# Attention tables of two heads built in one half: the odd head's and the next even head's

## The chip, the cores and the metric

One core of a Trainium2 chip runs the whole program. The metric is the device time of one execution in microseconds, the median of the runs shown. A step here is one pass of the attention loop, and n counts its (head, sequence) pairs.

## The reference

The input x is 8 sequences of 512 tokens by 128 channels. Three layers follow each other: half a mixture-of-experts layer, attention with 16 heads, and half a mixture-of-experts layer again. The change touches attention alone. For each head h and each sequence:

```python
q, k, v = cproj(Wq), cproj(Wk), cproj(Wv)            # complex, 64 wide
qr, kr = q * phase, k * phase                        # phase: cos and sin of t * omega[h]
E = exp(clip(-mu[h] * |t_i - t_j|, -30, 0))
s = real(qr . conj(kr)); qn = |q|^2; kn = |k|^2
V = sigma_sq/(2 mu) * (1 - E*E) + eta_sq + gamma_sq
maha = max(qn + E*E*kn - 2*E*s, 0) / V
logits = coef[h] * log1p(maha / nu) - 32 * log(V)    # masked to i >= j
out = softmax(logits) @ v                            # then times Wo, added to x
```

E and V depend on the head and on |i - j| alone, so each head has a few tables that serve all 8 sequences: the phases (cos and sin), the decay E, the threshold V (kept as `lam`), and the head's query and key weights split into a high and a low part for the fp32r matmuls.

## The kernel before

Attention is a software pipeline over 16 heads x 8 sequences = 128 pairs, written out in full for every engine. `steps` calls `a_step(i, r)` with n = 16 i + r: i counts pairs of heads, r = 0 to 7 are the steps of the even head 2i (the even half), r = 8 to 15 those of the odd head 2i+1 (the odd half). Scores are lower-triangular: four blocks of 128, 384, 512 and 256 columns lie side by side in 1280 columns (`ORDER`, `OFF`, `SW`).

In step n the engines work on different pairs:

- **TensorE** computes `scores(n)`, the squared norms of pair n+1 (`norms`), the projections of pair n+2 (`project`), turns the probabilities of pair n-1 (`turn`), and multiplies those of pair n-2 with the values (`weigh`). In an even half it also makes the values of both heads of the pair (`values`), 12 more matmuls. An odd half has none of these.
- **VectorE** (in the order of its program): `peaks(n-1)` (L1551, four custom instructions that read `u` and `lam`), half of `accumulate(n-3)` (L1583), `distances(n)` (L1560, which waits for the scores, then L1564), `query_norms(n+1)` (L1570), the other half of `accumulate`, `turn_parts(n+2)` (L1605 and L1607), `inverse(n-1)` (L1575), and last the step's share of the table building.
- **ScalarE**: `soften(n-1)` (L1356), `key_norms(n+1)` (L1364), `clamp(n)` (L1373), `turned_out(n-1)` (L1380), `logs(n)` (L1386), then the table building, `square(n+2)` (L1392) and in even halves `values_out` (L1399).
- **GpSimd**: `rotate(n+1)` (L1482), which waits for the scores of pair n and for the crossing DMA, then `spread(n+1)` (L1491, four pieces in `ORDER`, from `decay` and `knorm` to `ek`).
- **The sync queue** (SP): in every step the two crossing DMAs of pair n+2 (L1146, L1147), issued after L1605; besides these it loads the tables (`load`) and copies the decay (`expand`, L1137).

The table building of head h is placed by the step r mod 8 of the half before it:

```python
        FRONT, EXP, EXPAND, LN, MASK = 1, 2, 3, 4, 6
        def building(part, i, r):
            if r % B != part:
                return None
```

So the tables of an odd head are built in the even half before it, and those of an even head in the odd half before it. FRONT is a copy of the head's parameters (L1509) and dist x (-mu), clipped (L1511). EXP is ScalarE's high part of the weights (L1337) and the exponential (L1340). EXPAND is VectorE's low part of the weights (L1519) and the square of the decay (L1528), and on the sync queue three copies of the widest block of `decay` to the narrower ones. LN is ScalarE's logarithm into `lam` (L1347). MASK is L1535 and L1539 on `lam`. All tables have two buffers, chosen by the parity of the head; those of the even heads lie in the buffer `early`, which the profile prints for several of them.

Of the kernel before, what the change touches and what calls it, by code (L numbers as in the profile page):

```python
# [28 lines left out]
P = 128  # L29
# [1006 lines left out]
def attention_phase(nc, s):  # L1036
# [4 lines left out]
    with ExitStack() as ctx:  # L1041
# [3 lines left out]
        lam = (s.lam0, sb("lam1", [P, N]))  # L1045
        cos = (s.cos0, sb("cos1", [P, N]))
        sin = (s.sin0, sb("sin1", [P, N]))
        hp = (s.hp0, sb("hp1", [P, NPAR]))
# [14 lines left out]
        trig_in = (S["trig_in0"], S["trig_in1"])  # L1063
        block = ctx.enter_context(nc.Block())
# [4 lines left out]
        near = lambda I: slice((TILES - 1 - I) * P, N)  # L1069

# [28 lines left out]
        FRONT, EXP, EXPAND, LN, MASK = 1, 2, 3, 4, 6  # L1099
# [9 lines left out]
        def building(part, i, r):  # L1109

            if r % B != part:
                return None
            if isinstance(i, int) and not 0 < i * 2 + r // B + 1 < H:
                return None
            return r // B + 1

        @block.sync
        def _(sp):
            def load(i, off):
                h, par = i * 2 + off, off % 2  # L1120
                wait(sp, S["w_lo"], h)
                apart(sp, S["sp_passed"])
                wait(sp, S["cos_done"], (h - 1) * B)
                apart(sp, S["sp_passed"])
                sp.dma_start(wqk_raw[:], s.wqk[h]).then_inc(S["w_in"], 16)
# [5 lines left out]
            def expand(i, off):  # L1131

                h, par = i * 2 + off, off % 2
                wait(sp, S["decay_done"], h + 1)
                far = decay[par][:, span(TILES - 1)]
                for I in range(TILES - 1):
                    sp.dma_start(decay[par][:, span(I)], far[:, near(I)]).then_inc(S["expanded"], 16)  # L1137

            def a_step(i, r):
                c = r + 2  # L1140
                if live(i, c):
                    n = i * 16 + c
                    wait(sp, S["rot_done"], n)
                    apart(sp, S["sp_passed"])
                    wait(sp, S["bs_done"], n + 1)
                    sp.dma_start(crossed[0:DH, :], by_sin[DH:P, :]).then_inc(S["crossed_in"], 16)  # L1146
                    sp.dma_start(crossed[DH:P, :], by_sin[0:DH, :]).then_inc(S["crossed_in"], 16)  # L1147
                if building(FRONT, i, r):
                    load(i, building(FRONT, i, r))
                if building(EXPAND, i, r):  # L1150
                    expand(i, building(EXPAND, i, r))

            steps(nc.sync, a_step)
# [176 lines left out]
        def _(a):  # L1330
            def build(part, i, off):

                h, par = i * 2 + off, off % 2
                if part == EXP:
                    a.wait_ge(S["w_in"], h * 16 + 16)
                    wait(a, S["qk_done"], (h - 1) * B)
                    a.activation(wqk[par][0][:], wqk_raw[:], ACT.Copy).then_inc(S["w_hi"], 1)  # L1337
                    a.wait_ge(S["arg_done"], h + 1)
                    far = decay[par][:, span(TILES - 1)]
                    a.activation(far, far, ACT.Exp).then_inc(S["decay_done"], 1)  # L1340
                elif part == LN:
                    if h == 0:
                        a.wait_ge(S["decay_done"], 1)
                        a.activation(decay2[:], decay[0][:, span(TILES - 1)], ACT.Square).then_inc(S["decay2_done"], 1)
                    a.wait_ge(S["decay2_done"], h + 1)
                    wait(a, S["zred_done"], 2 * (h - 1) * B)
                    a.activation(lam[par][:], decay2[:], ACT.Ln, bias=hp[par][:, A_PLUS_B:A_PLUS_B + 1],  # L1347
                                 scale=hp[par][:, NEG_A:NEG_A + 1]).then_inc(S["lnv_done"], 1)
# [11 lines left out]
            def key_norms(i, r):  # L1360
                n, par = i * 16 + r, parity(r)
                wait(a, S["kn_done"], n + 1)
                wait(a, S["ek_done"], n)
                a.activation(knorm[:], s.p6[:], ACT.Identity,  # L1364
                             bias=hp[par][:, NEG_NU_A:NEG_NU_A + 1]).then_inc(S["norm_done"], 1)
# [16 lines left out]
            def logs(i, r):  # L1382
                n, par = i * 16 + r, parity(r)
                for k, (half, _) in enumerate(HALVES):
                    a.wait_ge(S["relu_done"], 2 * n + k + 1)
                    a.activation(u[:, half], u[:, half], ACT.Ln, bias=hp[par][:, U_MIN:U_MIN + 1]).then_inc(S["ln_done"], 1)  # L1386
# [39 lines left out]
            def a_step(i, r):  # L1426
# [14 lines left out]
                if i == 0 and r == -1:  # L1441
                    build(LN, 0, 0)
# [12 lines left out]
                for part in (EXP, LN):  # L1455
                    if building(part, i, r):
                        build(part, i, building(part, i, r))
# [12 lines left out]
        def _(g):  # L1470
            def build_first():
                g.wait_ge(S["lnv_done"], 1)
                apart(g, S["pool_passed"])
                g.tensor_scalar(lam[0][:], lam[0][:], hp[0][:, LAM_SCALE:LAM_SCALE + 1],
                                hp[0][:, NEG_LN_NU:NEG_LN_NU + 1], ALU.mult, ALU.add).then_inc(S["lam0_done"], 1)
# [29 lines left out]
        def _(v):  # L1505
            def build_front(i, off):
                h, par = i * 2 + off, off % 2
                wait(v, S["norm_done"], (h - 1) * B)
                v.tensor_copy(hp[par][:], s.params[:, bass.ds(h, 1), :].rearrange("p a c -> p (a c)")).then_inc(S["hp_done"], 1)  # L1509
                v.wait_ge(S["hp_done"], h + 1)  # L1510
                v.tensor_scalar(decay[par][:, span(TILES - 1)], s.dist[:, span(TILES - 1)], hp[par][:, NEG_MU:NEG_MU + 1],  # L1511
                                MIN_EXP, ALU.mult, ALU.max).then_inc(S["arg_done"], 1)

            def build_weights(i, off):

                h, par = i * 2 + off, off % 2
                v.wait_ge(S["w_hi"], h + 1)
                wait(v, S["qk_done"], (h - 1) * B)
                v.tensor_tensor(wqk[par][1][:], wqk_raw[:], wqk[par][0][:].bitcast(F32),  # L1519
                                ALU.subtract).then_inc(S["w_lo"], 1)  # L1520

            def build_square(i, off):

                h, par = i * 2 + off, off % 2
                far = decay[par][:, span(TILES - 1)]
                v.wait_ge(S["decay_done"], h + 1)
                v.wait_ge(S["lnv_done"], h)
                v.tensor_tensor(decay2[:], far, far, ALU.mult).then_inc(S["decay2_done"], 1)  # L1528

            def build_back(i, off):  # L1530

                h, par = i * 2 + off, off % 2
                if h > 0:
                    v.wait_ge(S["lnv_done"], h + 1)
                    v.tensor_scalar(lam[par][:], lam[par][:], hp[par][:, LAM_SCALE:LAM_SCALE + 1],  # L1535
                                    hp[par][:, NEG_LN_NU:NEG_LN_NU + 1], ALU.mult, ALU.add).then_inc(S["lam0_done"], 1)
                v.wait_ge(S["lam0_done"], h + 1)
                diag = lam[par][:, near(0)]
                v.scalar_tensor_tensor(diag, s.upper[:], hp[par][:, INV_COEF:INV_COEF + 1], diag,  # L1539
                                       ALU.mult, ALU.add).then_inc(S["lam_done"], 1)  # L1540

            def peaks(i, r):
                n, par = i * 16 + r, parity(r)
                v.wait_ge(S["lam_done"], i * 2 + r // B + 1)
                wait(v, S["exp_done"], n)
                wait(v, S["tr_done"], n)
                for k, (_, pieces) in enumerate(HALVES):
                    v.wait_ge(S["ln_done"], 2 * n + k + 1)
                    apart(v, S["dve_passed"])
                    for I in pieces:  # L1550
                        last = v.tensor_tensor_reduce(z[:, span(I)], u[:, span(I)], lam[par][:, near(I)],  # L1551
                                                      hp[par][:, NEG_COEF:NEG_COEF + 1], HIGHEST, ALU.add, ALU.min,
# [13 lines left out]
            def query_norms(i, r):  # L1566
                n, par = i * 16 + r, parity(r)
                wait(v, S["q2_done"], n + 1)
                wait(v, S["relu_done"], 2 * (n - 1))
                v.tensor_scalar(qnorm[:, r % 2, :], s.p5[:, 0:TILES], hp[par][:, NEG_NU_A:NEG_NU_A + 1], None,  # L1570
                                ALU.subtract).then_inc(S["qn_done"], 1)
# [135 lines left out]
            def a_step(i, r):  # L1707
# [27 lines left out]
                if building(FRONT, i, r):  # L1735
                    build_front(i, building(FRONT, i, r))
                if building(EXPAND, i, r):
                    build_weights(i, building(EXPAND, i, r))
                    build_square(i, building(EXPAND, i, r))
                if building(MASK, i, r):  # L1740
                    build_back(i, building(MASK, i, r))
                if i == 0 and r == -1:
                    late_refine()
                if i == 0 and r == 0:
                    build_back(0, 0)
# [15 lines left out]
def program(nc, args, out):  # L1761
    with ExitStack() as ctx:
# [24 lines left out]
        def part(n):  # L1787
# [6 lines left out]
        s.hp0 = part(NPAR)  # L1794
        s.late_var, s.late_root, s.late_rstd, s.late_shift = (part(2 * TILES) for _ in range(4))
# [7 lines left out]
                 "late_stat late_mv late_var late_ln late_root late_rstd late_step late_xn late_xt late_hi late_lo mv_done expanded")  # L1803
# [65 lines left out]
```

## Time and profile before

| | |
|---|---|
| median of 3 runs | 1714.13 us (1711.09 to 1719.28) |
| profiled execution, own time | 1711.93 us |
| its span | 1710.1 us |
| TensorE, share of the span busy | 97% |
| VectorE | 87% |
| ScalarE | 85% |
| GpSimd | 57% |
| mean granted TensorE clock | 0.998 |

The attention loop runs from about 261 to 1494 us of the span. A half is the eight intervals from one L1560 to the next, beginning with the L1560 of its first pair.

### The profile page before, as it was taken

To read this page: it belongs to the slowest core of one execution; us is meant where nothing else is said; L and a number is where in the kernel's file an instruction comes from. 1 tells how busy PE (TensorE), PEld (TensorE's weight loads), DVE (VectorE), ACT (ScalarE), POOL (GpSimd) and SP (SyncE) were. 2 spreads that over 40 slices of the span, in tenths; PEclk is the share of its full clock that TensorE was granted. 3 is DMA by queue.
4 is the path that set the end of the run, shared out by engine and by line. 5 is a ranking of instruction groups with operands and counts; after the bars stand their busy time and mean duration, and the time that the engine had idled before them with its cause. 6 is when DMAs were issued, how large, how long until landed. Compare 5 with 4: busy or idle time off the path is not lost. (4 is left out here: it accounts for less than half of the span.)

```text
span 1710.1 us, 30987 instructions
## 1 busy us (share of the span) xinstructions
PE 1650.9 (97%) x9690; PEld 1334.7 (78%) x9690; DVE 1488.8 (87%) x3380; ACT 1457.8 (85%) x2924; POOL 974.7 (57%) x826
## 2 busy tenths in 40 slices
PE   5999988999999999999999999999999999999998
PEld 4787866877887888788788778878887887777876
DVE  6878887899899989988998998899899989977675
ACT  6677678999999999999999999999998998766765
POOL 3554556565556556655665566556565655345565
PEclk9999999999999999999999999999999999999999
DMA  6000032232222323232322223232222222100000
GB/s 175 1 1 1 1 102 66 67 80 62 75 60 78 78 59 81 57 87 50 87 66 65 72 72 75 51 87 62 75 66 72 66 63 60 25 1 13 13 8 18
DMA packets 49475, 98.21 MB, mean 57 GB/s; under 512 B 8096, under 2 KB 25760, under 8 KB 49312
## 3 DMA queue, kind: packets, MB, share of 16 engines
q1 hardware_dynamic: 49312, 96.23, 22.0%
q8 instruction: 78, 1.28, 0.3%
q14 instruction: 85, 0.70, 0.1%
HBM read 17.95 MB, written 5.24 MB: 14 GB/s over the span
## 5 line engine op out<-in xcount | busy, mean ns | idle before, releaser
L1482 POOL TENSOR_TENSOR early<-early 128x1024 f32<-128x1024 f32 x127 | 303.4, 2389 | 483.3 <-PE pS L1162 258.2
L654 POOL TENSOR_TENSOR hid_lo_d<-hid_d,hid_hi_d 128x512 fp32r<-128x512 f32 x176 | 231.4, 1315 | 218.7 <-ACT hid_hi_d L559 212.1
L1373 ACT ACTIVATE early<-early,qnorm 128x128 f32<-128x128 f32 (+3 forms) x512 | 246.5, 553 | 71.8 <-DVE early L1564 70.6
L1162 PE MATMUL pS<-early 128*128 128x128 f32 (+3 forms) x1024 | 297.6, 433 | 0.3 <-PEq L105 0.3
L1356 ACT ACTIVATE early<-early,nmax 128x128 f32<-128x128 f32 (+3 forms) x512 | 281.2, 560 | 13.4 <-DVE nmax L1551 12.5
L1560 DVE SCALAR_TENSOR_TENSOR pS<-pS,ek 128x1280 f32<-128x1280 f32 x128 | 191.0, 1492 | 60.7 <-PE pS L1162 59.8
L1162 PEld LDWEIGHTS pS<-early 128*128 128x128 f32 x1024 | 164.7, 191 | 96.0 <-issue 61.4
L1491 POOL TENSOR_TENSOR ek<-early 128x128 f32<-128x128 f32 (+3 forms) x256 | 216.3, 878 | 3.8 <-ACT early L1364 2.9
L1491 POOL TENSOR_TENSOR ek<-decay,early 128x128 f32<-128x128 f32 (+3 forms) x256 | 215.5, 876 | 2.4 <-DVE pS L1560 2.4
L1177 PEld LDWEIGHTS pV<-ones,early 128*128 128x128 f32 x1016 | 134.2, 193 | 60.8 <-issue 60.8
L1207 PE MATMUL pS<-ident,early 128*128 128x128 f32 x1280 | 169.0, 275 | 12.4 <-DVE early L1564 8.3
L1207 PEld LDWEIGHTS pS<-ident,early 128*128 128x128 f32 x1280 | 146.0, 142 | 43.3 <-issue 17.7
L559 ACT ACTIVATE hid_hi_d<-hid_d 128x512 fp32r<-128x512 f32 x176 | 111.1, 631 | 60.8 <-DVE hid_d L787 42.8
L1380 ACT ACTIVATE probT<-pS 128x1280 f32<-128x1280 f32 x128 | 157.5, 1231 | 5.8 <-PE pS L1207 5.4
L1285 PE MATMUL p<-val_odd,probT 128*128 128x128 f32 x1280 | 155.3, 277 | 1.3 <-ACT probT L1380 1.3
L1583 DVE SCALAR_TENSOR_TENSOR x_sb<-p,rinv,x_sb 128x128 f32<-128x128 f32 x512 | 153.5, 341 | 1.4 <-PE p L1285 1.4
L1285 PE MATMUL p<-val_even,probT 128*128 128x128 f32 x1280 | 153.5, 275 | 0.0
L1285 PEld LDWEIGHTS p<-val_odd,probT 128*128 128x128 f32 x1280 | 147.9, 192 | 2.4 <-ACT probT L1380 1.6
L1285 PEld LDWEIGHTS p<-val_even,probT 128*128 128x128 f32 x1280 | 148.0, 192 | 0.1
L1551 DVE CUSTOM_DVE_ANT_0 early<-early,lam,hp 128x128 f32<-128x128 f32 (+3 forms) x256 | 131.6, 568 | 10.4 <-ACT early L1386 5.4
L1551 DVE CUSTOM_DVE_ANT_0 early<-early 128x128 f32<-128x128 f32 (+3 forms) x256 | 127.7, 554 | 14.4 <-ACT early L1386 12.7
L1175 PE MATMUL pV<-early,ones 128*128 128x512 f32 x254 | 131.9, 601 | 5.7 <-ACT val_odd L1399 4.0
(395 smaller groups left out, 3953.3 us busy)
## 6 DMA issues: line engine op xcount, KB each, us to landing
early<-early SPq DMA_DIRECT2D x256, 256.0 KB, 3.6
early<-trig_d SPq DMA_DIRECT2D x64, 64.0 KB, 2.0
trig_d<-early SPq DMA_DIRECT2D x3, 1024.0 KB, 6.9
early<-in_w SPq DMA_DIRECT2D x3, 704.0 KB, 8.8
x_sb<-in_x SPq DMA_DIRECT2D x4, 512.0 KB, 8.4
early<-in_wqk SPq DMA_DIRECT2D x16, 128.0 KB, 3.5
cos<-trig_d SPq DMA_DIRECT2D x32, 64.0 KB, 2.2
sin<-trig_d SPq DMA_DIRECT2D x32, 64.0 KB, 2.0
```

The source lines that it names most:

```text
L654: g.tensor_tensor(hid_lo[:, par], hid[:, par], hid_hi[:, par].bitcast(F32), ALU.subtract).then_inc(lo_done, 1)
L1162: last = pe.matmul(s.pS[:, span(I)], rot[:, I * P:(I + 1) * P], rot[:, N:N + (I + 1) * P], start=True, stop=True)
L1207: last = pe.transpose(s.pS[:, col:col + P], z[:, col:col + P], s.ident[:])
L1285: last = pe.matmul(s.p7[:, I * P:(I + 1) * P], turned[:, OFF[I] + J * P:OFF[I] + (J + 1) * P], val[:, J * P:(J + 1) * P], start=(J == 0), ...
L1356: last = a.activation(z[:, span(I)], z[:, span(I)], ACT.Exp, bias=nmax[:, I:I + 1], scale=-1.0, accum_out=rsum[:, r % 4, I:I + 1])
L1373: last = a.activation(u[:, span(I)], u[:, span(I)], ACT.Relu, bias=qnorm[:, r % 2, I:I + 1])
L1380: a.activation(probT[r % 2][:], s.pS[:, 0:SW], ACT.Copy).then_inc(S["trc_done"], 1)
L1482: g.tensor_tensor(rot[:], by_cos[:], crossed[:], ALU.add).then_inc(S["rot_done"], 1)
L1491: last = g.tensor_tensor(ek[:, span(I)], decay[par][:, span(I)], knorm[:, 0:(I + 1) * P], ALU.mult)
L1551: last = v.tensor_tensor_reduce(z[:, span(I)], u[:, span(I)], lam[par][:, near(I)], hp[par][:, NEG_COEF:NEG_COEF + 1], HIGHEST, ALU.add, A ...
L1560: v.scalar_tensor_tensor(s.pS[:, 0:SW], s.pS[:, 0:SW], -2.0, ek[:], ALU.mult, ALU.add).then_inc(S["w_done"], 1)
L1583: last = v.scalar_tensor_tensor(xt, s.p7[:, I * P:(I + 1) * P], rinv[:, r % 4, I:I + 1], xt, ALU.mult, ALU.add)
```

## The change

The tables of both the odd head 2i+1 and the next even head 2i+2 are now built in the steps of the even half (r = 1 to 8, and the load of the phases of the even head at r = 9). Each part has two places, the first for the odd head (`off` 1) and the second for the even head (`off` 2). While the even half runs, its own decay and threshold tables are in use, so the next even head gets `far_even` (512 columns) for the decay and a second `lam` buffer in the first 512 columns of `dist`; the decay is then copied to all four blocks of `decay[0]` at r = 8. The high part of the weights goes from ScalarE to VectorE (a `tensor_copy`, HALF), and the copy of the head's parameters goes: all read `s.params` in place. `peaks`, `key_norms`, `logs` and `query_norms` only change their operands so.

```diff
+        expanded = (S["expanded0"], S["expanded1"])
+        def lam(h):
+            return lam1[:] if h % 2 else lam_even[h // 2 % 2]
+        def far(h):
+            return decay[h % 2][:, span(TILES - 1)] if h % 2 or h == 0 else s.far_even
-        FRONT, EXP, EXPAND, LN, MASK = 1, 2, 3, 4, 6
+        FRONT, EXP, HALF, LOW, SQUARE, LN, MASK = (1, 2), (2, 3), (3, 6), (4, 7), (3, 5), (4, 6), (6, 7)
+        WEIGHTS, TRIG, EXPAND = (1, 5), (1, 9), (3, 8)
         def building(part, i, r):
-            if r % B != part:
-                return None
-            if isinstance(i, int) and not 0 < i * 2 + r // B + 1 < H:
-                return None
-            return r // B + 1
+            for off in (1, 2):
+                if r == part[off - 1] and i * 2 + off < H:
+                    return i * 2 + off
+            return None
...
+            def expand(h):
+                par = h % 2
                 wait(sp, S["decay_done"], h + 1)
+                apart(sp, S["sp_passed"])
+                wait(sp, S["t_done"], 2 * (h - 1) * B)
+                for I in range(TILES - par):
+                    sp.dma_start(decay[par][:, span(I)], far(h)[:, near(I)]).then_inc(expanded[par], 16)
...
-                    a.wait_ge(S["w_in"], h * 16 + 16)
-                    wait(a, S["qk_done"], (h - 1) * B)
-                    a.activation(wqk[par][0][:], wqk_raw[:], ACT.Copy).then_inc(S["w_hi"], 1)
...
-                    wait(a, S["zred_done"], 2 * (h - 1) * B)
+                    wait(a, S["zred_done"], 2 * (h - (1 if h % 2 else 3)) * B)
...
-                wait(g, S["expanded"], 48 * (i * 2 + r // B))
+                wait(g, expanded[par], 48 * (i + r // 16 + 1) if par else 64 * (i + r // 16))
...
-                v.tensor_copy(hp[par][:], s.params[:, bass.ds(h, 1), :].rearrange("p a c -> p (a c)")).then_inc(S["hp_done"], 1)
+                    wait(v, expanded[0], 64 * (h // 2 - 1))
...
+            def build_half(h):
+                v.wait_ge(S["w_in"], h * 16 + 16)
+                wait(v, S["qk_done"], (h - 1) * B)
+                v.tensor_copy(wqk[h % 2][0][:], wqk_raw[:]).then_inc(S["w_hi"], 1)
```

## Rows read from the trace of the kernel before

**Rows 1.** Windows, an odd half and the sum of seven: us, then busy (instructions) by engine, clock, DMA.
```profile
core 0: us, PE busy (x) PEld busy (x) DVE busy (x) ACT busy (x) POOL busy (x), PEclk, DMA share, GB/s
496.40:568.60 72.20, 71.18 (x433) 56.05 (x433) 70.49 (x158) 67.07 (x140) 45.60 (x40) 1.00 0.29 74
...
sum 508.90, PE 499.04 PEld 393.07 DVE 496.92 ACT 469.68 POOL 320.23; mean PE 71.29 PEld 56.15 DVE 70.99 ACT 67.10 POOL 45.75
```

**Rows 2.** Windows of the seven even halves between and behind them: the sum.
```profile
sum 560.90, PE 560.75 PEld 472.37 DVE 494.10 ACT 528.50 POOL 320.74; mean PE 80.11 PEld 67.48 DVE 70.59 ACT 75.50 POOL 45.82
```

**Rows 3.** Timeline of VectorE, odd half 496.4 to 568.6: L1560, once a step.
```profile
505.23 1.49 DVE L1560 SCALAR_TENSOR_TENSOR pS<-pS,ek 128x1280 f32<-128x1280 f32 x1
...
514.94 1.48 DVE L1560 SCALAR_TENSOR_TENSOR pS<-pS,ek 128x1280 f32<-128x1280 f32 x1
...
523.63 1.49 DVE L1560 SCALAR_TENSOR_TENSOR pS<-pS,ek 128x1280 f32<-128x1280 f32 x1
...
533.10 1.48 DVE L1560 SCALAR_TENSOR_TENSOR pS<-pS,ek 128x1280 f32<-128x1280 f32 x1
...
541.79 1.49 DVE L1560 SCALAR_TENSOR_TENSOR pS<-pS,ek 128x1280 f32<-128x1280 f32 x1
...
550.67 1.49 DVE L1560 SCALAR_TENSOR_TENSOR pS<-pS,ek 128x1280 f32<-128x1280 f32 x1
...
559.91 1.49 DVE L1560 SCALAR_TENSOR_TENSOR pS<-pS,ek 128x1280 f32<-128x1280 f32 x1
```

**Rows 4.** The same timeline, the first L1551 of the step that begins at 514.94.
```profile
521.22 0.35 DVE L1551 CUSTOM_DVE_ANT_0 early<-early,lam,hp 128x128 f32<-128x128 f32 x1 [0.21 <-issue]
```

**Rows 5.** Single lines of the building: ns minimum/median/maximum of one.
```profile
L1511 DVE TENSOR_SCALAR early<-dist,early x7: 485/487/905, 359.5 to 1274.0; 128x512 f32<-128x512 f32 x7
...
L1519 DVE TENSOR_TENSOR wqk_lo<-early,wqk_hi x15: 389/392/708, 300.4 to 1370.2; 128x256 fp32r<-128x256 f32 x15
...
L1528 DVE TENSOR_TENSOR early<-early x7: 677/679/1219, 377.5 to 1292.2; 128x512 f32<-128x512 f32 x7
...
L1535 DVE TENSOR_SCALAR early<-early x7: 514/517/1014, 404.3 to 1321.5; 128x512 f32<-128x512 f32 x7
...
L1539 DVE SCALAR_TENSOR_TENSOR early<-upper,early x8: 350/352/721, 266.4 to 1322.5; 128x128 f32<-128x128 f32 x8
...
L1347 ACT ACTIVATE early<-early x8: 799/802/813, 258.1 to 1304.6; 128x512 f32<-128x512 f32 x8
```

**Rows 6.** Timelines by engine in an even half, steps from 476.34 and 486.38.
```profile
476.34 1.50 DVE L1560 SCALAR_TENSOR_TENSOR pS<-pS,ek 128x1280 f32<-128x1280 f32 x1 [1.15 <-PE pS L1162]
...
486.38 1.50 DVE L1560 SCALAR_TENSOR_TENSOR pS<-pS,ek 128x1280 f32<-128x1280 f32 x1 [0.71 <-PE pS L1162]
...
478.66 1.93 ACT L1373 ACTIVATE early<-early,qnorm 128x128 f32<-128x128 f32 x4 [0.77 <-DVE early L1564]
...
476.48 2.38 POOL L1482 TENSOR_TENSOR early<-early 128x1024 f32<-128x1024 f32 x1 [4.33 <-PE pS L1162]
```

**Rows 7.** GpSimd and VectorE, odd halves: L1551 beside L1491, and beside L1482.
```profile
838.73 2.38 POOL L1482 TENSOR_TENSOR early<-early 128x1024 f32<-128x1024 f32 x1 [4.76 <-DMA early<-early]
841.07 3.34 POOL L1491 TENSOR_TENSOR ek<-decay,early 128x128 f32<-128x128 f32 x4
...
843.66 0.90 DVE L1551 CUSTOM_DVE_ANT_0 early<-early,lam,hp 128x128 f32<-128x128 f32 x1 [0.21 <-issue]
...
1294.81 2.38 POOL L1482 TENSOR_TENSOR early<-early 128x1024 f32<-128x1024 f32 x1 [1.99 <-DMA early<-early]
...
1294.78 2.69 DVE L1551 CUSTOM_DVE_ANT_0 early<-early,lam,hp 128x256 f32<-128x256 f32 x1
```

**Rows 8.** L1147, issue to landing: all 127, the one at 501.8, the one at 1312.0.
```profile
DMA to landing us min/median/max: 3.6/3.7/5.1
...
DMA to landing us min/median/max: 4.7/4.7/4.7
...
DMA to landing us min/median/max: 5.1/5.1/5.1
```

**Rows 9.** Timeline of the sync queue, the three decay copies of an odd half.
```profile
529.66 2.47 SPq L1137 DMA_DIRECT2D early<-early  x3
```

More of the change, by code:

```diff
@@ L1147, in a_step @@
                     sp.dma_start(crossed[DH:P, :], by_sin[0:DH, :]).then_inc(S["crossed_in"], 16)
-                if building(FRONT, i, r):
-                    load(i, building(FRONT, i, r))
+                if building(WEIGHTS, i, r):
+                    load_weights(building(WEIGHTS, i, r))
+                if building(TRIG, i, r):
+                    load_trig(building(TRIG, i, r))
                 if building(EXPAND, i, r):
-                    expand(i, building(EXPAND, i, r))
+                    expand(building(EXPAND, i, r))
             steps(nc.sync, a_step)
@@ L1330, in _, with build @@
         def _(a):
-            def build(part, i, off):
-                h, par = i * 2 + off, off % 2
+            def build(part, h):
                 if part == EXP:
-                    a.wait_ge(S["w_in"], h * 16 + 16)
-                    wait(a, S["qk_done"], (h - 1) * B)
-                    a.activation(wqk[par][0][:], wqk_raw[:], ACT.Copy).then_inc(S["w_hi"], 1)
                     a.wait_ge(S["arg_done"], h + 1)
-                    far = decay[par][:, span(TILES - 1)]
-                    a.activation(far, far, ACT.Exp).then_inc(S["decay_done"], 1)
+                    a.activation(far(h), far(h), ACT.Exp).then_inc(S["decay_done"], 1)
                 elif part == LN:
@@ L1441, in a_step @@
                 if i == 0 and r == -1:
-                    build(LN, 0, 0)
+                    build(LN, 0)
                 if i == 0 and r == 0:
@@ L1456, in a_step @@
                     if building(part, i, r):
-                        build(part, i, building(part, i, r))
+                        build(part, building(part, i, r))
                 if live(i, r + 2):
@@ L1537, in build_back @@
                 v.wait_ge(S["lam0_done"], h + 1)
[L1538 to L1540 removed]
+                diag = lam(h)[:, near(0)]
+                v.scalar_tensor_tensor(diag, s.upper[:], hp(h, INV_COEF), diag, ALU.mult, ALU.add).then_inc(S["lam_done"], 1)
             def peaks(i, r):
[L1543 removed]
@@ L1550, in peaks @@
                     for I in pieces:
-                        last = v.tensor_tensor_reduce(z[:, span(I)], u[:, span(I)], lam[par][:, near(I)],
-                                                      hp[par][:, NEG_COEF:NEG_COEF + 1], HIGHEST, ALU.add, ALU.min,
+                        last = v.tensor_tensor_reduce(z[:, span(I)], u[:, span(I)], lam(h)[:, near(I)],
+                                                      hp(h, NEG_COEF), HIGHEST, ALU.add, ALU.min,
                                                       nmax[:, I:I + 1])
@@ L1735, in a_step @@
                 if building(FRONT, i, r):
[L1736 to L1739, printed above, removed]
+                    build_front(building(FRONT, i, r))
+                if building(HALF, i, r):
+                    build_half(building(HALF, i, r))
+                if building(LOW, i, r):
+                    build_low(building(LOW, i, r))
+                if building(SQUARE, i, r):
+                    build_square(building(SQUARE, i, r))
                 if building(MASK, i, r):
-                    build_back(i, building(MASK, i, r))
+                    build_back(building(MASK, i, r))
                 if i == 0 and r == -1:
@@ L1794, in program @@
         s.hp0 = part(NPAR)
+        s.far_even = part(N)
         s.late_var, s.late_root, s.late_rstd, s.late_shift = (part(2 * TILES) for _ in range(4))
```

77 lines of the change are left out of this document (34 added, 43 removed).

## The prediction

> **What bounds the kernel now.** I read the windows first, one per half, because the change moves work from one kind of half to the other. The reader is to see that the two kinds have different limits. Seven even halves last 560.9 us, and TensorE is busy for 560.75 of them, 80.1 us a half [rows 2]. VectorE is busy for only 494.1, ScalarE for 528.5. Seven odd halves (those of heads 1 to 13, in which an even head's tables are built) last 508.9 us, 72.7 each, and there VectorE has 496.9, more than in the even halves, though the time is shorter [rows 1]. The last odd half, head 15's, builds nothing and is left out.
>
> The timeline then shows what an odd step costs. In the half from 496.4 to 568.6 the distances between one L1560 and the next are 8.83, 9.71, 8.69, 9.47, 8.69, 8.88, 9.24 and 8.69 us (the outer ends are those of the window) [rows 1, 3]. The three steps of 8.69 build nothing. In them VectorE idles 0.21 us before its first L1551, put down to issue, and nowhere else [rows 4]: this is VectorE's own work, the floor of an odd step. The other steps are longer by what is built in them. In an even step, VectorE instead stands still before L1560 until TensorE's scores are done, 1.15 us where nothing was built in the step before and 0.71 where MASK was [rows 6].
>
> **What the change takes out of the odd halves.** Against 8.69, the steps of that half are longer by 1.02 (FRONT), 0.78 (the low part and the square), 0.19 (ScalarE's logarithm, which delays L1386 and so L1551) and 0.55 (MASK) [rows 3]. The 1.02 is not typical: L1511 takes 905 ns there against its median of 487 [rows 5], 0.42 more, and the parameter copy before it was stretched likewise, so FRONT without such a stretch costs 0.3. That makes 0.3 + 0.78 + 0.19 + 0.55 = 1.8 us a half, 12.7 over seven.
>
> A half at its floor would be 8.83 + 7 x 8.69 = 69.7 us, seven of them 487.6. The trace has 508.9, so the excess is 21.3, of which building explains 12.7. The other 8.6 I read as follows. The crossing DMA L1147 lands after 3.7 us as a rule and after up to 5.1 [rows 8]. Asked one by one, 12 of the 49 that are issued in the first seven steps of these odd halves needed 4.6 or more, the first at 501.8, the last at 1312.0. A late landing makes GpSimd's L1482 and L1491 late. In the step that starts at 837.40, L1491 is at work until 844.41, and the first L1551, due at 843.66, takes 0.90 instead of 0.35; at 1294.8, L1482 is waiting or running when the fourth L1551 should, and that takes 2.69 [rows 4, 7]. So L1551 stands still until GpSimd's instruction ends. The Trainium skill's page "GPSIMD Engine Reference" (Key points) says the same: GpSimd shares its SBUF interfaces with VectorE, and contends with instructions that have two SBUF inputs or run in a 2-port mode. By that rule every building instruction is exposed too, and the trace agrees with 905 ns for L1511, 1219 for L1528 and 1014 for L1535.
>
> Does that 8.6 go as well? Only in part. The large stall of 2.2 us needs L1551 to be late enough to meet the next L1482: it stood in a step that builds. A step without building ends its L1551 before the next landing. But the small stall does not need building; it gets likelier, since GpSimd's start hangs on the landing, and a shorter step leaves less of it over. I keep 12 late landings and give each 0.6 us (0.90 - 0.35 = 0.55 from the row, a bit more for a landing of 5.1): 7.2 us. Seven odd halves then take 487.6 + 7.2 = 494.8, which is 14.1 less than 508.9.
>
> **What it adds to the even halves.** The VectorE shares by step are: r = 1 and 2 FRONT (0.49 each), r = 3 HALF and the square, r = 4 the low part, r = 5 the square, r = 6 HALF and the odd head's MASK, r = 7 the low part and the even head's MASK [rows 5]. The trace has no HALF. It lies between nothing (a step's idle time of 0.31 to 0.4 before L1551 can hide it) and 0.39, the row of the low part with the same 256 columns and two inputs; I take 0.3. The heaviest steps are then MASK plus 0.3 to 0.39. MASK alone brought the idle time before L1560 from 1.15 to 0.71 [rows 6], so 0.3 to 0.4 us is left even at r = 6 and 7, and TensorE does not notice. If this cover were gone, each us would cost 7 us over the halves.
>
> ScalarE loses the copy of the weights and gets a second exponential and a second logarithm, at r = 2, 3, 4 and 6. It waits 0.77 us for L1564 in each even step [rows 6]. The dearest of the four is the logarithm, 0.80 [rows 5], about 0.7 of it additional behind the instruction before it, one per step: hidden. I add nothing for the even halves.
>
> **Queues and waits.** On the sync queue the even head's copies are four instead of three and move from r = 11 to r = 8, where they stand behind that step's crossing DMAs. At 2.47 us for three [rows 9], four take 3.3, and the next crossing is issued 8.7 us after the last: no delay. The copies are first read at r = 15, by L1491. The new waits there (`t_done` of the even head's pairs, `decay_done`) were satisfied before the crossing DMA in front of them was. The weights go to r = 5, behind the low part of r = 4. FRONT's `expanded0` is from the half before. LN at r = 6 waits for the square of r = 5, MASK at r = 7 for that LN, each one step old. TensorE's `project` of the odd head's first pair (r = 6) needs the low part of r = 4, formerly r = 3: still before. All of this costs nothing, and nothing is queued behind a wait that lasts.
>
> **The sum** against the profiled execution's own 1711.9 us: 1711.9 - 14.1 = 1697.8. The median of the runs is 2.2 above it, so 1714.1 - 14.1 = 1700.0 us, 0.8% faster.
>
> **Rivals.**
> *A, GpSimd takes the place (no real change).* At 8.69 us a step, L1482 starts about 0.5 us after L1560 (landing 3.7 after an issue at about 5.5) and L1491 is done 5.7 later, at 6.3, which is just when L1551 starts (521.22 - 514.94 = 6.28 [rows 3, 4]). If landings in a run of short steps are later by 0.2 to 0.3, each step of the odd half would be that much longer: 49 x 0.2 = 10 us given back, 1710. For it speaks that the margin is nil; against it that steps of 8.69 stand right behind others of 8.69 to 8.97, and that a stalled step gives the next one the time back.
> *B, even halves slower (slower than before).* L1482 in an even half starts with the end of the scores (476.48, released by TensorE [rows 6]). If the added work at r = 6 and 7 pushes the last L1551 behind the end of the scores, L1551 is caught by L1482 and stands 2.2 us, as at 1294.8 [rows 7]. Twice in each of seven halves is 31 us: 1700 + 31 = 1731. It decides once the two steps lose more than the 1.1 to 1.3 us between the end of L1551 and L1560; the sum above uses 0.8.
> *C, the excess goes completely.* If late landings no longer meet L1551, 21.3 us are gained: 1693.
> *D, it doesn't do what it says:* the odd step has another floor near by, TensorE, with 71.2 busy of 72.2 [rows 1]. But that busy share stretches with the step; in the 8.69 steps L1560 is not released by TensorE [rows 3].
>
> **Chances.** Forecast 0.62, C 0.14, A 0.14, B 0.07, D 0.03. The forecast's own range is 1696 to 1704. The range for 8 in 10 reaches toward C and into A: 1693 to 1708. What a measurement of this kernel tells from no change is 0.5%, 8.6 us, so under 1705.5 is faster: forecast, C and a tenth of A and D, 0.78; same is most of A and D, 0.14; slower is B and a rest, 0.08.
>
> **What the profile after would show.** Odd halves of 69.7 to 71.5 us in the windows, with VectorE busy near 68.5 and no building line in them; even halves still 80.1 with TensorE busy throughout and VectorE at about 73; the idle time before L1560 at the steps after r = 6 and 7 down to 0.3 to 0.4, but there. The copy HALF near 0.3 us. L1551 durations over 0.35 only in steps behind a late landing. Wrong would be: even steps over 10.05, an L1551 of over 2 us in an even half, L1560 of an odd half released by TensorE or by GpSimd, or landings of L1147 above 4 us at r = 8 and 9, behind the copies.

## The result and the profile after

The changed kernel runs in 1696.9 us (median of 5 runs, 1695.6 to 1700.6), the kernel before in 1715.9 (5 runs, 1711.1 to 1719.6). The ratio is 0.9892, with a 95% interval of 0.9868 to 0.9916: 1.1% faster. The profiled execution took 1695.6 us, 16.3 less than the profiled one of before; 1697.8 was forecast against its own time, 1700.0 for the median.

The page of the kernel after, its first part (engine, busy time, share of the span, instructions):

```profile
span 1693.8 us, 30993 instructions
PE 1642.7 (97%) x9690; PEld 1337.0 (79%) x9690; DVE 1483.9 (88%) x3380; ACT 1452.4 (86%) x2909; POOL 974.3 (58%) x826
```

VectorE has as many instructions as before and 5 us less busy time; ScalarE has 15 fewer, the casts, and also 5 us less. So little work went away; the question is where it lies. The windows of the seven odd halves of the kernel after, with their sum (columns as in [rows 1]):

```profile
495.70:565.40 69.70, 69.70 (x433) 56.45 (x432) 67.62 (x152) 65.11 (x137) 45.59 (x40) 1.00 0.31 79
...
796.00:867.20 71.20, 70.51 (x433) 56.29 (x432) 69.11 (x153) 65.41 (x137) 45.65 (x40) 1.00 0.30 77
...
sum 493.10, PE 491.33 PEld 394.92 DVE 478.15 ACT 457.43 POOL 319.72; mean PE 70.19 PEld 56.42 DVE 68.31 ACT 65.35 POOL 45.67
```

and the sum of the seven even halves between and behind them:

```profile
sum 561.20, PE 561.06 PEld 473.31 DVE 506.20 ACT 533.91 POOL 320.73; mean PE 80.15 PEld 67.62 DVE 72.31 ACT 76.27 POOL 45.82
```

Against [rows 1] the odd halves are 15.8 us shorter and have 18.8 us less of VectorE. Against [rows 2] the even halves have taken on 12.1 us of VectorE and 5.4 of ScalarE, and last as long as before, 561.2 to 560.9. The odd halves are 15.8 of the 16.3 us.

The steps show it best. VectorE's timeline of the half that begins at 495.7, L1574 (L1560 before), where [rows 3] had 9.47, 8.69, 8.88 and 9.24 us between such rows:

```profile
521.92 1.50 DVE L1574 SCALAR_TENSOR_TENSOR pS<-pS,ek 128x1280 f32<-128x1280 f32 x1
530.63 1.49 DVE L1574 SCALAR_TENSOR_TENSOR pS<-pS,ek 128x1280 f32<-128x1280 f32 x1
539.33 1.49 DVE L1574 SCALAR_TENSOR_TENSOR pS<-pS,ek 128x1280 f32<-128x1280 f32 x1
548.03 1.49 DVE L1574 SCALAR_TENSOR_TENSOR pS<-pS,ek 128x1280 f32<-128x1280 f32 x1
```

Now 8.70 follows on 8.70. In the even half, the two fullest steps (r = 6 from 475.63, r = 7 from 485.67), with what VectorE builds in them:

```profile
481.62 0.27 DVE L1531 CAST wqk_hi<-early 128x256 fp32r<-128x256 f32 x1
481.80 0.54 DVE L1550 TENSOR_SCALAR lam<-lam,params 128x512 f32<-128x512 f32 x1
485.67 1.50 DVE L1574 SCALAR_TENSOR_TENSOR pS<-pS,ek 128x1280 f32<-128x1280 f32 x1 [0.49 <-PE pS L1183]
491.66 0.40 DVE L1537 TENSOR_TENSOR wqk_lo<-early,wqk_hi 128x256 fp32r<-128x256 f32 x1
491.97 0.54 DVE L1550 TENSOR_SCALAR early<-early,params 128x512 f32<-128x512 f32 x1
495.70 1.50 DVE L1574 SCALAR_TENSOR_TENSOR pS<-pS,ek 128x1280 f32<-128x1280 f32 x1 [0.36 <-PE pS L1183]
```

The idle time in front of the scores was 1.15 and 0.71 us in [rows 6]; it is down to 0.49 and 0.36, but there: TensorE still releases VectorE, not the other way about.

What is left above 8.70 in the odd halves is the stall that [rows 7] showed, L1565 (L1551 before) behind GpSimd. The longest of the kernel after, GpSimd first, then VectorE:

```profile
833.39 2.41 POOL L1495 TENSOR_TENSOR early<-early 128x1024 f32<-128x1024 f32 x1 [4.96 <-DMA early<-early]
835.73 3.41 POOL L1504 TENSOR_TENSOR ek<-decay,early 128x128 f32<-128x128 f32 x4
...
837.77 0.78 DVE L1565 CUSTOM_DVE_ANT_0 early<-early,lam,params 128x128 f32<-128x128 f32 x1 [0.21 <-issue]
...
838.49 1.07 DVE L1565 CUSTOM_DVE_ANT_0 early<-early,lam,params 128x384 f32<-128x384 f32 x1
```

L1495 waited for a landing that took 5.1 us, L1504 runs to 839.14, and two pieces of L1565 take 0.78 and 1.07 instead of 0.35 and 0.61. Twelve instructions of L1565 in these seven halves are stretched so, by 4.6 us together; none takes more than 1.08, and the 2.69 of [rows 7] has no successor.

### The profile page after: what moved, and what is told of

It reads as the page before. It is cut to its first block and busy times, and to the rows that moved or that the text cites. A ratio compares the mean times of both kernels' runs of the same rounds, so it can differ in the third digit from the quotient of the medians.

```text
span 1693.8 us, 30993 instructions
## 1 busy us (share of the span) xinstructions
PE 1642.7 (97%) x9690; PEld 1337.0 (79%) x9690; DVE 1483.9 (88%) x3380; ACT 1452.4 (86%) x2909; POOL 974.3 (58%) x826
## 3 DMA queue, kind: packets, MB, share of 16 engines
q1 hardware_dynamic: 50320, 98.07, 22.5%
## 5 line engine op out<-in xcount | busy, mean ns | idle before, releaser
L1495 POOL TENSOR_TENSOR early<-early 128x1024 f32<-128x1024 f32 x127 | 303.2, 2387 | 470.0 <-PE pS L1183 258.6
L1574 DVE SCALAR_TENSOR_TENSOR pS<-pS,ek 128x1280 f32<-128x1280 f32 x128 | 191.4, 1495 | 55.3 <-PE pS L1183 54.4
L1504 POOL TENSOR_TENSOR ek<-early 128x128 f32<-128x128 f32 (+3 forms) x256 | 216.7, 881 | 3.6 <-ACT early L1379 3.0
L1504 POOL TENSOR_TENSOR ek<-decay,early 128x128 f32<-128x128 f32 (+3 forms) x256 | 215.3, 876 | 0.0
L1400 ACT ACTIVATE early<-early,params 128x512 f32<-128x512 f32 (+1 forms) x256 | 196.9, 819 | 0.0
L1228 PE MATMUL pS<-ident,early 128*128 128x128 f32 x1280 | 164.5, 274 | 5.1 <-DVE early L1578 3.1
L1565 DVE CUSTOM_DVE_ANT_0 early<-early,lam,params 128x128 f32<-128x128 f32 (+3 forms) x256 | 130.8, 567 | 13.8 <-issue 11.2
```

Of the source, the lines that this page charges most:

```text
L1228: last = pe.transpose(s.pS[:, col:col + P], z[:, col:col + P], s.ident[:])
L1400: a.activation(u[:, half], u[:, half], ACT.Ln, bias=hp(h, U_MIN)).then_inc(S["ln_done"], 1)
L1495: g.tensor_tensor(rot[:], by_cos[:], crossed[:], ALU.add).then_inc(S["rot_done"], 1)
L1504: last = g.tensor_tensor(ek[:, span(I)], decay[par][:, span(I)], knorm[:, 0:(I + 1) * P], ALU.mult)
L1574: v.scalar_tensor_tensor(s.pS[:, 0:SW], s.pS[:, 0:SW], -2.0, ek[:], ALU.mult, ALU.add).then_inc(S["w_done"], 1)
```

## The experiments

All start from the changed kernel. Ratios are to the kernel before, run beside each; the changed kernel itself has 0.9892 (0.9868 to 0.9916). "Odd halves" is the sum over heads 1 to 13, 508.9 us before and 493.1 after; "even halves" the sum over heads 2 to 14, 560.9 and 561.2. The runs were taken in three groups. The median of the kernel before was 1713.7, 1713.8 and 1716.9 us in them, against 1715.9 above, and the changed kernel was not run again in them, so a difference of its 1696.9 from a run of another group is uncertain by some 2 us.

### The placement alone, and a part of it

```diff
-        FRONT, EXP, HALF, LOW, SQUARE, LN, MASK = (1, 2), (2, 3), (3, 6), (4, 7), (3, 5), (4, 6), (6, 7)
-        WEIGHTS, TRIG, EXPAND = (1, 5), (1, 9), (3, 8)
+        FRONT, EXP, HALF, LOW, SQUARE, LN, MASK = (1, 9), (2, 10), (2, 10), (3, 11), (3, 11), (4, 12), (6, 14)
+        WEIGHTS, TRIG, EXPAND = (1, 9), (1, 9), (3, 11)
```

> The changed kernel with the even head's parts put back into the odd half (r = 9 to 14, the decay copies at r = 11); the new buffers, the cast on VectorE and the parameters read in place stay. Theory (the gain is the placement): each odd half gets its building back, about 0.25 + 0.07 + 0.78 + 0.19 + 0.55 = 1.85 us, 13 over seven, and with it some long stalls of L1565: 1710 to 1714, odd halves of 72 to 73 us, even halves 80.1. Rival (one of the other edits made the gain): within 3 us of the changed kernel's 1697, odd halves of 70 to 71.

Measured: 1711.7 us, ratio 0.9983 (0.9966 to 1.0). The windows of the odd halves:

```profile
sum 510.60, PE 500.36 PEld 394.50 DVE 499.04 ACT 467.44 POOL 321.52; mean PE 71.48 PEld 56.36 DVE 71.29 ACT 66.78 POOL 45.93
```

They are back where [rows 1] had them, 510.6 for 508.9, and the even halves still have 561.1. The new buffers, the cast on VectorE and the parameters read in place are all in this kernel and are worth 0.2% together, by the interval at most 0.34%. The placement is the gain.

With only the logarithm and MASK of the even head put back:

```diff
-        FRONT, EXP, HALF, LOW, SQUARE, LN, MASK = (1, 2), (2, 3), (3, 6), (4, 7), (3, 5), (4, 6), (6, 7)
+        FRONT, EXP, HALF, LOW, SQUARE, LN, MASK = (1, 2), (2, 3), (3, 6), (4, 7), (3, 5), (4, 12), (6, 14)
```

> The changed kernel with only the even head's logarithm and MASK back in the odd half (r = 12 and 14). Theory: these steps grow by 0.19 and 0.55 us as before the change, 0.74 x 7 = 5.2: 1701 to 1703. Rival (the gain came from the whole being away, for instance from stalls that any building causes): more than 10 us back, or none.

Measured: 1702.9 us, ratio 0.9941 (0.9921 to 0.9962), odd halves 499.2, which is 6.1 more, for 5.2 expected. The median steps of r = 13 and 14 are 8.88 and 9.25, as before the change, the others 8.70 and the first, r = 8, 8.81, as in the changed kernel. A part put back costs its part.

### The same work added on either side

Four multiplications of 512 columns (0.66 us each) per half, into a spare buffer; in the even halves the condition is `r in (1, 2, 4, 5) and i > 0`:

```diff
+                if r in (10, 11, 12, 13) and i < 7:
+                    wait(v, spare_done, spares[0])
+                    v.tensor_tensor(spare[:], s.dist[:, span(TILES - 1)], s.dist[:, span(TILES - 1)],
+                                    ALU.mult).then_inc(spare_done, 1)
+                    spares[0] += 1
```

> The changed kernel with one more VectorE multiplication of 512 columns, of the kind of the decay's square (0.67 us), into a spare buffer at each of r = 10, 11, 12 and 13 of the seven odd halves of heads 1 to 13. Theory (an odd step is as long as VectorE's own work): each adds 0.6 less the 0.21 of idle time before L1565, so 0.4, 1.6 a half, 11 in all, less up to 3 for late landings that then meet a longer step: 1705 to 1709. Rival (TensorE or GpSimd sets the odd step): 1697 to 1700.

> The same multiplication, as often, at r = 1, 2, 4 and 5 of the even halves of heads 2 to 14. Theory (even halves are TensorE's, VectorE has 0.77 to 1.15 us idle before L1574 in these steps): 1697, no change within 0.2%, even halves still 80.1, that idle time smaller by 0.2 to 0.6. Rival (VectorE's total or its meetings with GpSimd count wherever they are): 1705 to 1709.

In the odd halves: 1707.9 us, ratio 0.9970 (0.9952 to 0.9988), 11.0 above the changed kernel's median; odd halves 505.9 in the profile, with one half of 76.4 to which I come back below. Its median steps are 9.26 at r = 10 and 8.98 at r = 11 to 13, against 8.70 to 8.71: that is 1.4 us a half and 9.7 of the 11. In the even halves: 1699.7, ratio 0.9915 (0.9892 to 0.9937), even halves 561.2. The 2.8 us in the second number are not in the even halves, but that kernel also had three of the multiplications in the steps behind the last pair, which I had not meant. So once more without those:

> The run with extra multiplications at r = 1, 2, 4 and 5 once more, now without the three that also fell into the steps behind the last pair. Theory: the even halves cost nothing, 1697 within 0.2%; what the first run had above 1697 came from those three or from the spread of the runs. Rival (VectorE's work in even halves costs a little, 0.1 us each): 1700.

Measured: 1697.7 us, ratio 0.9885 (0.986 to 0.991), even halves 561.0. The same 28 instructions cost some 10 us in the odd halves and nothing in the even ones. The profiles also show what the three at the end cost. From the last L1577 to the end of the span it is 230.6 us with them and 228.5 without, and 228.6 in the changed kernel (L1574).

### How near the edge r = 7 is

The same multiplication at r = 7, three times and once (`for k in range(3)` or `range(1)` around the lines above, with `r in (7,) and i < 7`).

> The same multiplication three times at r = 7, the fullest step of the even half, in each of the seven even halves before heads 1 to 13. That is 1.8 to 1.9 us more, where 0.36 is left before L1574 and some 0.25 before TensorE's transposes wait. Theory with the stall of rival B (a late L1565 meets L1495, which starts with the end of the scores, and stands until it ends): 1.2 us plus about 2.2 a half, 20 to 25 in all, 1717 to 1722, one L1565 a half of over 2 us. Without such a stall: 1.2 us a half, 1705 to 1706.

> The changed kernel with the 512-column multiplication once, not three times, at r = 7 of the seven even halves before heads 1 to 13: 0.6 us, where 0.36 is left before L1574 and about 0.25 behind it. Theory (rival B decides only where the last L1565 starts behind the end of the scores): nothing to 0.3 us a half, 1697 to 1699, no L1565 over 1.1 us in an even half. Rival (the even half is already at the edge, any more at r = 7 is caught by L1495): 2 us and more a half, 1711 and above.

Three times: 1733.1 us, ratio 1.0109 (1.0082 to 1.0136), slower than before the change. Once: 1697.9, ratio 0.9885 (0.9855 to 0.9914), none of its L1568 over 1.1 us, six of the even halves 0.1 to 0.2 longer each (the step r = 7 takes 10.19 us for 10.04). The step r = 7 from 487.98 of the kernel with three lasts 14.0 us. GpSimd and VectorE in it (L1498 is its L1495, L1507 its L1504, L1568 its L1565, L1577 its L1574):

```profile
498.16 2.41 POOL L1498 TENSOR_TENSOR early<-early 128x1024 f32<-128x1024 f32 x1 [3.83 <-PE pS L1186]
503.67 1.42 POOL L1507 TENSOR_TENSOR ek<-decay,early 128x128 f32<-128x128 f32 x2 [3.10 <-DVE pS L1577]
...
498.26 2.86 DVE L1568 CUSTOM_DVE_ANT_0 early<-early,dist,params 128x512 f32<-128x512 f32 x1
...
501.98 1.48 DVE L1577 SCALAR_TENSOR_TENSOR pS<-pS,ek 128x1280 f32<-128x1280 f32 x1
```

The scores end, GpSimd starts at 498.16 and works until 500.57, and the third L1568, which comes 0.1 us later, ends at 501.12, after 2.86 us where 0.75 is usual. That is rival B, made to happen: it begins between one and three such multiplications, 0.6 and 1.9 us of VectorE's work, away from the changed kernel.

What it costs has two parts. The step r = 7 takes 13.76 us in the median instead of 10.04, 3.7 more for 3.4 expected, or some 26 over seven. The rest is TensorE's clock. In two of the seven halves it stays at 1.00 and the next step is 8.69 us, no longer than in the changed kernel (8.81), although GpSimd waits there too for the late L1577:

```profile
347.22 1.48 DVE L1577 SCALAR_TENSOR_TENSOR pS<-pS,ek 128x1280 f32<-128x1280 f32 x1
355.91 1.49 DVE L1577 SCALAR_TENSOR_TENSOR pS<-pS,ek 128x1280 f32<-128x1280 f32 x1
```

In the other five the granted clock falls and the next step takes 9.70 to 10.90 us, 7 us more in all. Windows in the first of these halves to keep it and in the first to lose it (columns as in [rows 1]):

```profile
348.00:352.00 4.00, 2.28 (x18) 2.06 (x19) 3.96 (x8) 3.17 (x8) 3.09 (x4) 1.00 0.01 4
504.00:508.00 4.00, 3.52 (x18) 3.31 (x19) 4.00 (x8) 3.24 (x6) 3.00 (x4) 0.63 0.02 5
```

26 and 7 make the 33 us by which this profiled execution is longer than that of the changed kernel; the medians differ by 36. The 20 to 25 that were expected had the stall nearly right and the clock not at all.

### Moving a landing, and moving L1565 against it

Two small DMAs ahead of the crossing in the odd steps:

```diff
                     wait(sp, S["bs_done"], n + 1)
+                    if i < 7 and 8 <= r <= 14:
+                        for k in range(2):
+                            at = (i * 7 + r - 8) * 8 + 4 * k
+                            sp.dma_start(spare[:, at:at + 4], s.ident_d[:, 0:4]).then_inc(spare_in, 16)
                     sp.dma_start(crossed[0:DH, :], by_sin[DH:P, :]).then_inc(S["crossed_in"], 16)
```

> The changed kernel with two small DMAs (2 KB each, into a spare buffer) issued on the sync queue ahead of the crossing DMAs in the steps r = 8 to 14 of seven odd halves, so that the crossing is issued about 1 us later; nothing else waits for them. Theory (the margin between a landing and L1565 is nil in a step of 8.69 us): with landings 1 us later L1495 starts at about 1.2 us of the step, L1565 stands 0.4 us in nearly every one of 49 steps, 15 to 22 us: 1712 to 1719. Rival (late landings are hidden, the excess of the odd halves has another cause): 1697 to 1699.

Measured: 1713.8 us, ratio 1.0008 (0.9994 to 1.0021), odd halves 511.0. The whole gain is gone, with the tables still where the change put them. The first step that meets a later landing, one that itself took 3.8 us (L1501 is its L1495, L1510 its L1504, L1571 its L1565):

```profile
354.15 2.39 POOL L1501 TENSOR_TENSOR early<-early 128x1024 f32<-128x1024 f32 x1 [4.76 <-DMA early<-early]
356.50 3.40 POOL L1510 TENSOR_TENSOR ek<-decay,early 128x128 f32<-128x128 f32 x4
...
358.66 0.64 DVE L1571 CUSTOM_DVE_ANT_0 early<-early,lam,params 128x128 f32<-128x128 f32 x1 [0.21 <-issue]
...
359.24 1.07 DVE L1571 CUSTOM_DVE_ANT_0 early<-early,lam,params 128x384 f32<-128x384 f32 x1
```

In the profile 49 of its L1571 are stretched, by 22.5 us in all. So the margin of an odd step is nil, as rival A had it, and the landings decide. The crossing is issued 6.2 to 6.3 us after L1580 (its L1574) in most of these steps, 5.4 in the changed kernel, so 0.9 us later. Landings did not get later by themselves in the changed kernel: median 3.7 and maximum 5.1 as in [rows 8].

The other way, the first half of accumulate ahead of peaks in the odd steps, so that L1565 comes later against GpSimd:

```diff
+                early_add = i < 7 and 9 <= r <= 15
+                if early_add:
+                    accumulate(i, r - 3, range(TILES // 2))
                 if live(i, r - 1):
                     peaks(i, r - 1)
...
-                    if live(i, r - 3):
+                    if live(i, r - 3) and not early_add:
                         accumulate(i, r - 3, range(TILES // 2))
```

> The changed kernel with the first half of accumulate put ahead of peaks in the steps r = 9 to 15 of the odd halves of heads 1 to 13, so that L1565 comes 0.5 us later against GpSimd's L1495 and L1504, with the same work on VectorE. Theory (what is left above 8.69 in the odd steps is L1565 standing still behind GpSimd after late landings, 493.1 against 487.6 us over seven halves): most of 5.5 us goes, 1692 to 1694. Rivals: the wait for the previous weigh on TensorE (its end is at about 6.3 us of the step, VectorE would be there at 6.07) costs 0.2 us in each of 49 steps, 10 us: 1702 to 1707; or no effect: 1697.

Measured: 1696.3 us, ratio 0.9903 (0.9883 to 0.9924), odd halves 492.8. Both sides of the expectation came, smaller, and cancel: the stretched L1565 fall from 12 to 6 and from 4.6 to 2.1 us, and each step grows from 8.70 to 8.75, because the addition now waits for TensorE's product:

```profile
519.25 0.61 DVE L1596 SCALAR_TENSOR_TENSOR x_sb<-p,rinv,x_sb 128x128 f32<-128x128 f32 x2 [0.26 <-PE p L1306]
```

### What stands behind VectorE in an odd step

```diff
-                    if live(i, r - 3):
+                    if live(i, r - 3) and not (i < 7 and 9 <= r <= 15):
                         accumulate(i, r - 3, range(TILES // 2))
```

> The changed kernel without the first half of accumulate (two of the four additions into x, 0.5 us) in the steps r = 9 to 15 of the odd halves of heads 1 to 13: that part of the attention output is not added. Theory A (TensorE is right behind VectorE in the odd step, 8.63 us from one scores to the next): the step falls from 8.70 to 8.63 to 8.65 only, and L1565 meets GpSimd's L1504 as before, so 3 to 6 us less in all: 1691 to 1694. Theory B (VectorE has the odd step alone): 0.5 us in each of 49 steps, 20 to 25 us: 1672 to 1677.

Measured: 1689.1 us, ratio 0.9833 (0.9809 to 0.9856), odd halves 486.4. Two successive rows of L1574 in an odd half:

```profile
520.75 1.50 DVE L1574 SCALAR_TENSOR_TENSOR pS<-pS,ek 128x1280 f32<-128x1280 f32 x1 [0.26 <-PE pS L1183]
...
529.38 1.50 DVE L1574 SCALAR_TENSOR_TENSOR pS<-pS,ek 128x1280 f32<-128x1280 f32 x1 [0.26 <-PE pS L1183]
```

The step is 8.63 us, and TensorE releases L1574: of 0.5 us taken away, 0.07 shows in the step. The measured gain of 7.8 us is a little above the 3 to 6 expected, since the idle 0.26 also takes up part of the stretched L1565 and the first step of each half falls from 8.81 to 8.62. So a step of the changed kernel without a late landing is within 1% of TensorE's own pace in both kinds of half.

### The cast

HALF on ScalarE again, at r = 3 and 6:

```diff
+                if part == HALF:
+                    a.wait_ge(S["w_in"], h * 16 + 16)
+                    wait(a, S["qk_done"], (h - 1) * B)
+                    a.activation(wqk[h % 2][0][:], wqk_raw[:], ACT.Copy).then_inc(S["w_hi"], 1)
...
-                for part in (EXP, LN):
+                for part in (EXP, HALF, LN):
```

> The changed kernel with the high part of the weights back on ScalarE (at r = 3 and 6, 0.40 us) instead of VectorE's cast (0.27). Theory: ScalarE's 0.77 us of waiting in an even step takes r = 3 nearly whole and overruns at r = 6 (0.7 + 0.3) by 0.25, which TensorE does not feel, since the softened rows are there 2 us before the transposes: 1697 within 0.2%. Rival (ScalarE's time in even halves is on the path, so moving the cast was part of the gain): 2 to 4 us slower.

Measured: 1700.7 us, ratio 0.9926 (0.9904 to 0.9948). Six of the even halves last 80.3 to 80.4 instead of 80.1 to 80.2, all of it at r = 7 (10.23 us): ScalarE, which also has the logarithm at r = 6, does overrun. With the first half that is 1.5 us. Another 2.0 us of this profile lie before attention, which begins at 263.1 us instead of 261.1, and they are not the cast's: the granted clock is 0.58 in the window 37.5 to 41 and 0.54 in 157 to 164, where the changed kernel has 1.00, and the same two falls and the same 2.0 us stand in the profiles of two kernels above with the cast on VectorE, those with the four multiplications in the odd halves and, the second time, in the even ones. So the rival is right that ScalarE's time reaches the path, for 1.5 us where it had 2 to 4; what else the median of 3.8 holds is open, and the intervals overlap. With two heads' tables in one half, ScalarE has no room for the cast, and moving it to VectorE belongs to the change.

## Why the prediction was right

**The building leaves the bound.** The step on which all rested, that an odd step is VectorE's own work and an even step TensorE's, is shown from both sides: 28 equal instructions cost some 10 us in odd halves and nothing in even ones. The 12.7 us of building were counted well: undisturbed odd halves are 8.81 + 7 x 8.70 = 69.7 us, and a part put back costs 6.1 for 5.2.

**What is left of the stalls** was put at 12 late landings of 0.6 us, 7.2. Asked as for [rows 8], 8 of 49 were over 4.4 us, and the seven halves have 493.1 - 487.9 = 5.2 us over their floor. This term was sized too large by 2.0 us, which, less 0.3 for the floor (487.9 for 487.6), is the difference between 494.8 and 493.1. The price was right and the count was not: each of the 8 late landings is followed by a step with a stretched L1565, by 0.26 to 0.88 us and 0.57 in the mean, where 0.6 was taken, and no other step of these halves has one. That there were 8 and not 12 is luck. The same count is 7 to 15 in the other profiles, leaving out the one whose crossings are issued later; what a late landing goes with is told at the end. In the medians, 1696.9 for a forecast of 1700.0, the kernel before had moved too, from 1714.1 to 1715.9 with two more runs. That long stalls would go with the building holds in the one profile of after. In the odd halves they came back in the two runs that had the most VectorE work there (one of 2.60 us in each), and in no other.

**The even halves at nothing** is right, with 0.36 us to spare at the fullest step where 0.3 to 0.4 was forecast; the cast is 0.27 where I took 0.3. I had called ScalarE's share hidden. It is, but by less than I thought, as the run with the cast shows.

**Queues and waits.** No engine of the changed kernel stood over 0.3 us for a moved table, and the decay copies land after 2.3 to 3.7 us. One sign that I had named for being wrong did come: three of the crossing's landings at r = 9, behind the copies, took 4.6 us. It was a poor sign. The kernel before has two of 4.6 us at r = 9, and three of 4.6 to 5.1 at r = 8, with no copies there.

**The rivals.** A did not come, but its mechanism is real and close: crossing DMAs issued 0.9 us later undo the gain. B did not come; it begins between 0.6 and 1.9 us of further VectorE work at r = 7, where the working had 1.1 to 1.3 less 0.8, and its price of 2.2 a stall fits the stall itself (2.1), but it left out that TensorE's clock can fall behind it: the half with three multiplications took 3.7 us more where the clock held and about 5 where it fell. C is what the odd halves would have given with no late landing, 5.2 us more. D is wrong for the kernel after, but TensorE is only 0.07 us behind, as the stretched busy share in [rows 1] could not show.

## What to carry to other kernels

When halves of a loop have different bounds, look at the engine with idle time in each, and move what is not tied to a place into the half where it is covered; the gain is its duration less the idle time that it already filled. Before moving, find the fullest step and measure how much idle time is left in it, and ask what meets what if it runs over: here 0.6 us more in the fullest step cost 0.15 us, and 1.9 us more cost 3.7, or about 5 where the clock fell. A schedule in which two engines share a path to the memory has a second limit, the start of the other engine's work, and a transfer that lands a microsecond later can cost as much as the change brought.

## What the runs showed of the hardware

**A VectorE instruction that reads two tensors from SBUF stands until GpSimd's running instruction has ended; one that has begun is not disturbed, nor is one with an operand in PSUM.** L1568 at 498.26 stood 2.1 us behind an instruction that had started 0.1 earlier. In the first half of the same kernel the same piece began 0.14 us ahead of GpSimd's and took its usual 0.75, and the next piece stood:

```profile
343.50 0.75 DVE L1568 CUSTOM_DVE_ANT_0 early<-early,params 128x512 f32<-128x512 f32 x1
343.64 2.84 POOL L1498 TENSOR_TENSOR early<-early 128x1024 f32<-128x1024 f32 x1 [4.33 <-PE pS L1186]
...
344.17 2.59 DVE L1568 CUSTOM_DVE_ANT_0 early<-early,params 128x256 f32<-128x256 f32 x1
```

In the thirteen traces 255 of these pieces took over 0.05 us more than the median of their form. 254 of them began while a GpSimd instruction ran, and in 234 the delay is what was left of that instruction less 0.2 us; the other 20 began within 0.13 us of its end and stood through the next one as well. A lead of 0.03 us, as at 1294.78 in [rows 7], was not enough; with 0.07 to 0.7 us, none of these pieces was stretched. L1560, which reads `pS` from PSUM and overlaps L1482 in most steps, never took more than 1.50 us in 128. Two tensors are not a condition for all: L1511, which reads one, took 901 and 905 ns the two times that it came while GpSimd worked, and 485 to 489 else.

**A long stall can bring the clock down.** In the kernel with the four multiplications in the odd halves, one such stall of 2.1 us left TensorE idle for 3.11 us. Its windows around that place, and TensorE's first instruction after it:

```profile
828.00:832.00 4.00, 3.05 (x16) 2.02 (x14) 4.00 (x9) 1.69 (x5) 2.38 (x1) 1.00 0.00 0
832.00:836.00 4.00, 1.84 (x9) 1.78 (x10) 3.97 (x7) 3.17 (x9) 2.50 (x3) 0.63 0.00 0
836.00:840.00 4.00, 4.00 (x21) 4.00 (x20) 3.72 (x9) 3.47 (x5) 0.84 (x2) 0.51 0.52 131
```

```profile
834.16 2.15 PE L1231 MATMUL pS<-ident,early 128*128 128x128 f32 x9 [3.11 <-DVE early L1581]
```

The granted clock goes from 1.00 to 0.51, which is the 1.2 GHz level, and after the step of 12.37 us the next takes 10.81. This half lasts 76.4 us where the other six have 71.0 to 72.3. The run with the placement undone has such a half too (75.7 us, clock 0.98). The stalled step is 3.1 us over the median of its kind and the next 1.8, so a stall of 2 us costs nearly 5 when the clock falls. It does not always fall. Ten such stalls in the attention loops of the traces (one before the change, one with the placement undone, one here, seven with three multiplications at r = 7) left TensorE idle for 2.8 to 3.3 us, and the clock fell at seven of them. It held at the one of [rows 7], where the step takes 12.39 us and the next 8.69. What decides it was not found. The falls may be part of why the runs spread more with the placement undone, 1705 to 1717 us against 1696 to 1701 for the changed kernel; this was not tried by itself.

**A late landing goes with a packet of the instruction queue.** Of the 127 second crossing DMAs (L1147, after the change L1166), 19 landed after 4.5 to 5.1 us before the change and 13 after it, the others after 3.6 to 4.4; late ones lie in both kinds of half. The DMA view of the 5.2 us behind the issue at 828.2 in the kernel after, the one that took 5.1 us and made the longest stall there, has a packet of another queue beside the 160 of the crossing:

```profile
q1 hardware_dynamic: 160, 0.52, 41.1%
q8 instruction: 1, 0.02, 1.1%
```

The queue q8, of the kind that the profile calls instruction, moves 78 packets of 16 KB in the span, before and after the change. In the thirteen traces together, 181 of 1651 landings took over 4.4 us, and a q8 packet was under way during every one of them. Where the packet began 2.0 to 2.7 us behind the issue of L1166 (or its like), the landing was late in 167 cases of 167. So the late landings, and with them the stalls that are left in the odd halves, hang on where these packets fall. That is a coincidence without an exception, but no run moved the packets, so the cause is argued and not shown.
